# Four PSUM banks for the experts' inner values, and three chunks between ACT's scaling and its rounding, in an attention and mixture-of-experts kernel

## What is computed

```
h = layernorm(x) * (1 + ca) + sa              # sa..gb come from silu(c) @ wmod
x = x + ga * linear_attention(h)              # phi = elu + 1, causal, head size 64
h = layernorm(x) * (1 + cb) + sb
n = layernorm(h, rn_g, rn_b)
top_w, top_idx = top_k(n @ router_w.T + router_b, 2); top_w = softmax(top_w)
for e in range(8):                            # 2 experts for each token
    u = layernorm(h, ln_g[e], ln_b[e])
    u = gelu(u @ w1[e] + b1[e])               # 256 -> 1024 inner values
    u = u @ w2[e] + b2[e]                     # 1024 -> 256
    out += combine[e] * u
x = x + gb * out
```

## Time and profile before

| | |
|---|---|
| median of 3 runs | 1141.53 us (1140.14 to 1142.62) |
| time of the profiled execution | 1140.76 us |
| its span, first to last instruction | 1139.0 us |
| PE busy (matmul) | 991.4 us, 87% |
| DVE busy | 874.9 us, 77% |
| ACT busy | 629.8 us, 55% |
| POOL busy | 575.4 us, 51% |
| mean granted TensorE clock | 0.941 |

### The profile page before, as it was taken

The page is one execution under the profiler, slowest core; times in us unless marked ns, Lnnn a source line. Parts: engine busy times, 40 slices in busy tenths (PEclk is TensorE's granted clock), DMA queues, the critical chain, the costliest instruction groups (busy, mean ns, idle before and its releaser), DMA issues.

```text
span 1139.0 us, 32684 instructions
## 1 busy us (share of the span) xinstructions
PE 991.4 (87%) x8083; PEld 793.3 (70%) x8084; DVE 874.9 (77%) x2878; ACT 629.8 (55%) x1356; POOL 575.4 (51%) x479
## 2 busy tenths in 40 slices
PE   5878889887467788888999999999999999999986
PEld 2545565555456666666888888888888888888864
DVE  7779998887867677667877778787777878777875
ACT  3668877765656656664454454545445454544553
POOL 3125766676575355553545454454545445454442
PEclk8889988888569999999999999999999999999999
DMA  5333544333875675754444454544434444444442
GB/s 173 90 90 122 165 153 131 131 113 116 217 217 144 121 166 107 170 86 95 62 79 72 68 84 76 93 75 83 74 66 77 74 82 72 77 82 77 79 76 36
DMA packets 172037, 118.92 MB, mean 104 GB/s; under 512 B 111900, under 2 KB 158664, under 8 KB 171960
## 3 DMA queue, kind: packets, MB, share of 16 engines
q0 software_dynamic: 32832, 54.88, 24.2%
q1 hardware_dynamic: 139128, 63.13, 23.5%
HBM read 78.01 MB, written 45.98 MB: 109 GB/s over the span
## 4 chain that ended last, share of the span: by engine, by line
PE 52%; DVE 7%; issue 6%; ACT 5%; SPq 1%; ACTq 0%; POOLq 0%; DVEq 0%; DMA 0%
PE banks L1533 26%; PE banks L1545 25%; DVE store L1184 2%; ACT xT L694 2%; ACT store L731 1%; ACT gf L702 1%; DVE xT L1379 1%; DVE store L1440 1%; DVE store L1438 1%; DVE rowbuf L1416 1%; DVE rowbuf L1426 1%; DVE nhl L1386 1%; ACT store L709 1%; SPq L431 0%; SPq L437 0%
## 5 line engine op out<-in xcount | busy, mean ns | idle before, releaser
L1533 PE MATMUL banks<-nhl,store 128*128 128x256 bf16 (+1 forms) x3408 | 454.6, 269 | 48.6 <-ACT gf L702 26.0
L1545 PE MATMUL banks<-store 128*128 (+1 forms) x3240 | 450.4, 274 | 8.6 <-DVE store L1440 8.0
L702 ACT ACTIVATE gf<-banks,b1t 128x256 f32<-128x256 f32 (+1 forms) x568 | 255.4, 460 | 353.7 <-PE banks L1533 341.0
L641 POOL DMA_INDIRECT out<-rowbuf,ydst x135 | 226.4, 1677 | 362.0 <-DVE rowbuf L1426 324.0
L1533 PEld LDWEIGHTS banks<-nhl,store 128*128 (+1 forms) x3408 | 318.5, 98 | 113.8 <-issue 64.4
L1545 PEld LDWEIGHTS banks<-store 128*128 128x128 bf16 x3240 | 307.9, 98 | 60.6 <-issue 13.7
L1440 DVE TENSOR_TENSOR store<-gf,store 128x256 bf16<-128x256 f32 (+1 forms) x568 | 233.8, 412 | 69.7 <-ACT store L709 52.7
L1438 DVE CAST store<-gf 128x256 bf16<-128x256 f32 (+1 forms) x492 | 146.9, 299 | 118.8 <-ACT gf L702 98.2
L599 POOL DMA_INDIRECT lists<-store,slot x128 | 137.5, 1074 | 80.0 <-DVE store L1117 45.8
L607 POOL DMA_INDIRECT csB<-y_rows,ygb x135 | 138.9, 1029 | 41.9 <-issue 41.9
L694 ACT ACTIVATE xT<-xT,gb 128x256 f32<-128x256 f32 (+1 forms) x142 | 76.0, 582 | 31.6 <-DVE xT L1379 29.7
(11 more groups left out here) (247 smaller groups left out, 1041.7 us busy)
## 6 DMA issues: line engine op xcount, KB each, us to landing
vk<-lists SPq DMA_DIRECT2D x256, 64.0 KB
b2t<-in_L_ffn_b SPq DMA_DIRECT2D x71, 128.0 KB
store<-in_L_attn_x SPq DMA_DIRECT2D x16, 512.0 KB, 5.2
out<-store SPq DMA_DIRECT2D x16, 512.0 KB, 3.2
store<-in_L_ffn_w SPq DMA_DIRECT2D x28, 256.0 KB
store<-in_L_ffn_w SPq DMA_DIRECT2D x7, 1024.0 KB, 8.5
csB<-mod_rows SPq DMA_DIRECT2D x16, 256.0 KB, 4.3
csB<-y_rows,ygb POOLq DMA_INDIRECT x135, 3.7
```

Of the source, the lines that this page charges most:

```text
L641: g.indirect_dma_start(out_rows, bass.IndirectOffsetOnAxis(ap=ydst[:, r, h:h + 1], axis=0), yt[:, r, h, :], None, compute_op=ALU.add).then ...
L702: a.activation(gf[:, c % 4, 0:halves(j) * P], hidden(j)[c % 2][:, 0:halves(j) * P], ACT.Gelu, bias=b1t[:, r, c:c + 1]).then_inc(gf_s, 1)
L1533: last = t.matmul(hidden(j)[c % 2][:, 0:halves(j) * P], w, nhl[:, r, m, 0:halves(j) * P], start=n == 0, stop=n == 5)
L1545: last = t.matmul(ACC[r][h][:, 0:D], g[:, c, h * P:(h + 1) * P], w, start=c == 0 and n == 0, stop=c == NI - 1 and n == 2)
```

## The change

1. `MM` becomes four banks, 0, 1, 6 and 7, and chunk c uses `MM[c % 4]`. `first(c)` waits for `gf_s` of chunk c - 4 where it waited for c - 2. `MM0` and `hidden` go.
2. Tile 0 uses the same four banks. PE therefore waits ahead of it for the last router transpose (`nT_s`), ahead of its f2 for the last logits (`lg_s`) and ahead of its f3 for the last ranks (`base_s`). The last two waits stood ahead of tile 1.
3. `head_rows` is cut up. ACT's first scaling stays behind chunk 1, the second stands behind chunk 2, and the rounding behind chunk 3. At the end of the first part the four scalings of tiles 0 and 1 stand ahead of both roundings.
4. DVE's `split_rows` stands behind chunk 5 instead of chunk 3.

```diff
-        MM = bank[6:8]
-        MM0 = bank[4:6]
+        MM = (bank[0], bank[1], bank[6], bank[7])
...
-            def head_rows(j, half, r):
-
-                act.wait_ge(turn_s, j + 1)
+            def scale_rows(j, r, k):
+
+                if k == 0:
+                    act.wait_ge(turn_s, j + 1)
+                    hold(act, "act")
+                cols = slice(0, halves(j) * P)
+                a.activation(xT[:, r, k, cols], xT[:, r, k, cols], ACT.Identity, bias=gb4[:, r, 2 + k:3 + k], scale=gb4[:, r, k:k + 1]).then_inc(hx_s, 1)
+
+            def head_rows(j, r):
+
                 wait_past(act, mm1_s, NI * (j - 1))
+                act.wait_ge(hx_s, NK * j + NK)
                 cols = slice(0, halves(j) * P)
-                hold(act, "act")
-                for k in range(NK):
-                    a.activation(xT[:, r, k, cols], xT[:, r, k, cols], ACT.Identity, bias=gb4[:, r, 2 + k:3 + k], scale=gb4[:, r, k:k + 1]).then_inc(hx_s, 1)
-                act.wait_ge(hx_s, NK * j + NK)
                 a.activation(nhl[:, r, 0:NK, cols], xT[:, r, :, cols], ACT.Copy).then_inc(nh_s, 1)
...
-                    if c == 1 and not (isinstance(j, int) and (j == 0 or j + 1 >= TILES)):
-                        head_rows(j + 1, half + r, 1 - r)
+                    if not (isinstance(j, int) and (j == 0 or j + 1 >= TILES)):
+                        if c in (1, 2):
+                            scale_rows(j + 1, 1 - r, c - 1)
+                        if c == 3:
+                            head_rows(j + 1, 1 - r)
...
-                    if c == 3 and not first and not last_tile:
+                    if c == 5 and not first and not last_tile:
                         split_rows(j + 1, half + r, 1 - r)
...
             def first(j, r, s, c):
 
-                wait_past(pe, gf_s, NI * j + c - 1)
+                wait_past(pe, gf_s, NI * j + c - 3)
...
-                        last = t.matmul(hidden(j)[c % 2][:, 0:halves(j) * P], w, nhl[:, r, m, 0:halves(j) * P], start=n == 0, stop=n == 5)
+                        last = t.matmul(MM[c % 4][:, 0:halves(j) * P], w, nhl[:, r, m, 0:halves(j) * P], start=n == 0, stop=n == 5)
...
+                pe.wait_ge(nT_s, NB)
...
             for c in range(NI):
+                if c == 2:
+                    pe.wait_ge(lg_s, NB)
+                if c == 3:
+                    pe.wait_ge(base_s, NB)
+                    hold(pe, "pe")
                 tile_chunk(0, 0, 0, True, own, own, c)
```

More of the change, by code:

```diff
@@ L265, in halves @@
             return TH if not isinstance(j, int) or j < FULL else 1
-        def hidden(j):
-            return MM0 if isinstance(j, int) and j == 0 else MM
         def halves_to(n):
@@ L701, in gelu_chunk @@
                 wait_past(act, gl_s, NI * j + c - 3)
-                a.activation(gf[:, c % 4, 0:halves(j) * P], hidden(j)[c % 2][:, 0:halves(j) * P], ACT.Gelu, bias=b1t[:, r, c:c + 1]).then_inc(gf_s, 1)
+                a.activation(gf[:, c % 4, 0:halves(j) * P], MM[c % 4][:, 0:halves(j) * P], ACT.Gelu, bias=b1t[:, r, c:c + 1]).then_inc(gf_s, 1)
             def round_chunk(j, c):
@@ L821, in step @@
                     for q in range(2):
-                        head_rows(q, 0, q)
+                        for k in range(NK):
+                            scale_rows(q, q, k)
+                    for q in range(2):
+                        head_rows(q, q)
                 if i > NB + 2:
@@ L1572, in tile @@
                 pe.wait_ge(nl_s, j + 1)
-                if isinstance(j, int) and j == 1:
-                    pe.wait_ge(lg_s, NB)
-                    pe.wait_ge(base_s, NB)
                 if isinstance(j, int) and j in READY:
```

## The result

| | before | after |
|---|---|---|
| median of the runs | 1141.84 us (4 runs) | 1096.93 us (1093.84 to 1100.10, 4 runs) |
| time of the profiled execution | 1140.76 us | 1100.10 us |
| its span | 1139.0 us | 1098.3 us |
| PE busy | 991.4 us, 87% | 980.1 us, 89% |
| DVE busy | 874.9 us, 77% | 891.4 us, 81% |

The ratio is 0.961, with a 95% interval of 0.958 to 0.964. Every term of the forecast for tiles 0 to 14 came out within half a microsecond. Nearly all that was missed is in the loop.

What follows compares the result with a forecast made beforehand. PE was taken to bound the loop, a chain through ACT and DVE the early tiles. Gains 0.5 + 7.1 + 4.0 + 2.0 + 1.7 + 3.6 + 2.1 = 21.0 us gave 1120.5 us, range 1110 to 1131.

Steps and rivals of the forecast that it cites:

- tiles 1 to 4: Early tiles: chunk 4 on DVE comes sooner, tile 1 takes 13.61 us; together a gain of 4.0 us.
- tiles 5 to 12: Early tiles with two weight pieces: 12.30 us instead of 13.19, ending by a late split_rows; together 7.1 us.
- Tile 13: Early tile with one weight piece, ending by chunk 4 and s4: 11.17 us, a gain of 2.0 us.
- tile 14: Last weight rest comes 1.11 + 0.60 us sooner, its 3.17 us distance to PE's loop stays: gain 1.7 us.
- A: Rival, early tiles: split_rows is not late and they end by chunk 4; 1107.5 us, chance 0.07.
- B: Rival, early tiles: ACT's moved instructions delay later roundings, so the chain gets no shorter; 1135.4 us, chance 0.08.
- The banks: Four banks: nothing by themselves in early tiles, 0.5 us with tile 0; by the skill's rule alone about 1117 us.
- The loop: 45 loop tiles: ACT's block no longer delays chunk 2, 0.08 us each, together 3.6 us.
- My own step on DVE: Loop tiles: chunk 5 starts near 8.4 us, split_rows done near 9.4, some 1.1 us ahead of the next f0.
- Rival C: PE's clock: new idle time ahead of f0 halves the speed in 13 more tiles, giving back 21 us; 1141, chance 0.04.
- The end: Waits from 1080 us on: half, at f4, go for 2.1 us; the others, at f0, stay.
- D: Rival, slower: split_rows becomes the last wait in the loop too; 1160 us, chance 0.08.

Runs made afterwards that it cites:

- e1: The changed kernel with ACT's and DVE's orders of before, so only the four banks remain; 1141.84 us, ratio 0.9986.
- e4: The changed kernel with the two banks of before, both new orders kept; 1100.02 us, ratio 0.962.
- e8: The changed kernel with split_rows behind chunk 3 everywhere and ACT's rounding ahead of its weight head; 1084.51 us, ratio 0.950.

## Why the prediction was wrong

**Tiles 0 to 14: right, term by term.** Tile 0 gave 0.37 (0.5 forecast), tiles 1 to 4 4.1 (4.0, tile 1 13.57 against 13.61), tiles 5 to 12 6.8 (7.1). Of these, six took 12.26 to 12.31 where 12.30 was forecast. Tiles 5 and 7 gained 0.06 and 1.29. Tile 13 took 11.19 (11.17) and tile 14 gave 2.0 (1.7). The wait ahead of f0 is for split_rows, as forecast, and DVE's idle time ahead of chunk 1 is 2.37 (about 2.1 forecast). There was a little luck in the 12.30: split_rows came 0.22 us sooner than forecast (11.29 against 11.51), and f0 stood 0.29 us behind its end and not 0.1. Rivals A and B fall.

**The banks: right, against the rule.** I gave them nothing in the early tiles, and their run alone (e1) gave 1141.84 against 1142.48. The Trainium skill (Perfetto Trace Analysis, Matmuls) has independent groups rotate through banks, by which the time would have been about 1117, the prediction's estimate. No run with the banks alone shows that gain. Here the bank wait was the first sign of a chain through ACT and DVE. With the bank free, PE waits for the next link instead. The 2.1 us at the end that I gave them came with the orders too (e4).

**The loop: the step that failed.** The forecast said: "PE bounds the loop, and only 0.07 us a tile is left to gain in tile 31", and "45 tiles at 0.08 are 3.6". The delays at f4 did go, but they cost only the 24 tiles between the turns something, 0.08 each and 1.9 us together: without them a turn's tile stayed at 11.56 (e1). What the term left out are the 1.08 us (11.56 - 10.48) at each of 23 turns, 24.7 us. The forecast had two tiles of the loop 0.15 us shorter, and they went from 22.12 to 20.96. Tile 31 was read from its f0 to the next f0, and it is the first tile of a turn. The second, tile 32, was never read. Yet two rows on record pointed to it: the earlier trace rows show f0 of tile 31 with [0.77 <-issue], idle time for no wait that the profile shows, and PE's busy 384.9 of 400 us in the earlier trace rows leaves 15.1 us idle in some 36 tiles, 0.4 a tile and not 0.07. The earlier trace rows even hold the price: at the first turn of all PE starts 1.95 us after the end of the last weight rest, behind 2.02 us of idle time. I wrote "That distance stays", which was right there, because the rest is late. In the loop the same distance counts from chunk 4, and chunk 4 moved from 9.45 to 7.68.

My own step on DVE gave the answer and I did not draw it. It put chunk 5 "near 8.4" (8.33 measured) and split_rows done "near 9.4" (9.36 measured). Only f0 was checked against them, not the sequencer. The Trainium skill (Perfetto Trace Analysis, Sequencer Loop) has a matmul pushed into a queue where it waits for its semaphores while the sequencer reads on, by which the loads would have been done ahead in either kernel. That holds for a wait that stands on the matmul or its weight load, as in tiles 0 to 4 of this trace. In the loop the wait of s4 stands on the sequencer's register work, and with chunk 4 late the branch of tile 32 started 0.38 us after chunk 4's end and not before.

**Clock and end.** Rival C fell: PEclk is 0.98 from 335 to 534 us, with waits for split_rows of up to 1.5 us. Tile 15 kept its clock (granted 1.00, 10.50 us) behind 1.49 us of idle PE, where the kernel before had 0.86 and 12.15 us behind 2.02. In the six profiles whose clock was lower in tile 15, PE had been idle for 2.02 to 2.61 us ahead of it, but in e8 the clock held behind 2.13. So the 1.65 us of tile 15 are the clock's. The end gave 2.9 (2.1). There the forecast's "the others stand at f0 ... and stay" held: PE is still idle 0.47 to 0.58 us ahead of f0 of tiles 65 to 70 (0.48 to 0.57 before). Half tiles 64 to 69 take 7.41 us in the mean (7.5 forecast, 7.94 before). **D**, split_rows late in the loop, fell: it ends 1.1 us ahead of f0.

## What to carry to other kernels

When a loop's tiles are priced, read one whole turn and set busy time against the stretch. A few hundredths of idle time in one tile and 4% in the stretch don't fit together, and an idle time for "issue" at the head of a turn has a price and a condition of its own. Control work (branch, register loads) cost PE nothing here while its sequencer was ahead, so the question is which wait is the last ahead of it, whether it stands on the sequencer, and how early it is met. A faster producer can be worth more than the wait that the profile puts down to it. And where a wait heads the list, ask what the chain's next link does before a buffer is added.

## What the runs showed of the hardware

- Loading three numbers from SBUF into PE's registers took 0.77 to 0.78 us at the median, two 0.53 to 0.55, five 1.23: about 0.23 for each more. The branch of a turn took 0.21 us.
- From tile 5 on, where the weights' place came from a register, the wait ahead of a `second` stood on the sequencer's register work, and in tiles 0 to 4 on the weight load. In the loop of the kernel before it started 0.04 us after chunk 4's end, and the branch 0.38 after.
- From the end of the operation that PE's last wait of a turn stands for to the first matmul of the next turn were 2.09 us with three numbers (2.04 to 2.25 over the late turns of the table's kernels) and 2.55 with five.
- The gain hangs little on the chip among most of them (ratios 0.958 and 0.961 for the changed kernel), but on one chip the kernel before was 13 us longer than on the others. Why was not tried.
